# Token gather of a mixture-of-experts block: rows staged through HBM against quarter rows gathered straight to the DVE transpose, with the low part of h moved from POOL to DVE

## The chip, the cores and the metric

One Trainium2 chip, one core. The time is the device time of one execution in microseconds (us). Engines are named as the profile names them: PE (TensorE matmul), PEld (its weight loads), DVE (VectorE), ACT (ScalarE), POOL (GpSimd), SP (SyncE, which only issues DMAs here).

## The reference

Sixteen sequences of 256 tokens with 512 features go through a gated cross attention and then through a gated mixture of 8 experts with the two best experts of each token. Cut to what matters:

```python
x = x + tanh(g_xattn) * attention(layernorm(x), ctx, Wq, Wkv)
xn = layernorm(x)
probs = softmax(xn @ gate_w + gate_b, axis=1)          # over the tokens
vals, idx = top_k(probs, 2)
h = relu(xn @ w1[e] + b1[e]); h = relu(h @ w2[e] + b2[e]); y = relu(h @ w3[e] + b3[e])
v[e] = sum over the tokens of y * w_tok                # w_tok: vals where e was chosen, else 0
out = x + tanh(g_ffn) * (ind @ v)                      # ind: 1 where e was chosen
```

## The kernel before

All products are made in a split form: each operand is written as a high part (rounded to fp32r) and a low part (the rest), and PE adds three products, high x high, high x low and low x high (`split_product`, lines 1314 to 1323). So every operand needs one pass that writes the high part, on ACT, and one that subtracts it from the original, on DVE or POOL.

The attention and the gate run over the 16 sequences, up to about 400 us. Each token's two choices get a slot in a list sorted by expert; POOL scatters pairs (token number, weight) into `slot_pair` in HBM (`send_pairs`). Then the experts run over tiles of 352 slots of one expert. A table on the chip gives each tile's expert and first slot (`table`). There are 24 tiles here: the first (0 to 3) are interleaved with the end of the attention, and from tile 2 on a loop with a run-time count does the rest (`tile_pipeline`, lines 85 to 90: body(j) for j from 2, the last four tiles unrolled). In body(j) each engine has its own fixed order:

- PE (lines 1606 to 1619): layer 2 of tile j, layer 1 of tile j+1, layer 3 of tile j, each in two halves of 24 matmuls of 128x352.
- ACT (888 to 897): high part of w2 (third weights, `split_w(2, j)`), ReLU and high part of layer 2's result (`relu(1, j)`: per half two ReLUs to `h`, L837, and one copy to `h_hi`, L843), high part of the next w1 (`split_w(1, j+1)`), `relu(0, j+1)`, high part of the first weights (`split_w(0, j+2)`, L826) and of the activations (`et_high(j+2)`, L854).
- DVE (1272 to 1284): low parts of the three weights (`w_low`, L938, 128x2048), the transpose of the gathered rows (`transpose_blocks`, L1196), `weights_of` (L1213, L1214), the low part of the activations (L1202), and `weighted_sum(j)` (L1224 four times from PSUM, then L1229, L1232, L1236), which ends in the semaphore part_done.
- POOL (699 to 705): low part of h, `h_low(1, j)` and `h_low(0, j+1)` (L675, four instructions a tile), then `gather(j+3)`: three indirect DMAs (L665) of 128, 128 and 96 rows of 2 KB from the normalised activations `xn2_dram` to `xg`.
- SP (544 to 561): weight and bias loads (`load_w` loads only where the expert differs from the tile before), and for tile j+3 `store_rows` (L532, L533: `xg` to `rows_dram` in HBM), `load_idx(j+4)` (L491) and `load_quarters(j+3)` (L542: four DMAs from `rows_dram` to `xq`). All of it is one queue in this order, each entry behind its own waits.

`xq` holds 32-row blocks: partition q*32+b, block g holds quarter q of row g*32+b. The DVE transpose of 32x32 blocks then gives `et`, features on partitions and slots along the free dimension. Only tiles from BY_BLOCKS = 4 on go this way; PE transposes tiles 0 to 3 from `xg`. There is one `xq`, one `et` and one `et_hi`/`et_lo`. Layer 1 of tile m waits for the low parts of its weights and activations and for part_done of tile m-2 (line 1505), because it writes the PSUM banks that the weighted sum reads. Layer 3 waits for `h_lo` of layer 2, and layer 2 for `h_lo` of layer 1.

Of the kernel before, what the change touches and what calls it, by code (L numbers as in the profile page):

```python
# [71 lines left out]
NQ = P // QB  # L72
BY_BLOCKS = 4
# [24 lines left out]
def flamingo_block(nc, x, x_t, ctx_t, g_xattn, g_ffn, wq_t, wk_t, wv, gate_w, gate_b,  # L98
# [10 lines left out]
    rows_dram = nc.dram_tensor("rows_dram", (TILE, D), F32).ap()  # L109
# [4 lines left out]
    with ExitStack() as ctx:  # L114
# [124 lines left out]
        with ExitStack() as ph:  # L239
# [26 lines left out]
            et = alloc(ph, "et", [P, DC, TILE], F32)  # L266
            h_hi, h_lo = [h_hi0, h_hi1], [h_lo0, h_lo1]
# [81 lines left out]
        rows_out, xq_in, et_ready = sem("rows_out"), sem("xq_in"), sem("et_ready")  # L349
# [53 lines left out]
        def _(sp):  # L403
# [122 lines left out]
            def store_rows(m):  # L526
                need(sp, gathered, 16 * TH * (m + 1))
                wait_alone(sp, "sp")
                need(sp, xq_in, 16 * NQ * (m - BY_BLOCKS))
                wait_alone(sp, "sp")  # L530
                full = TILE // P
                sp.dma_start(rows_dram[0:full * P].rearrange("(c p) d -> p c d", p=P), xg[:, 0:full]).then_inc(rows_out, 16)  # L532
                sp.dma_start(rows_dram[full * P:], xg[0:TILE - full * P, full]).then_inc(rows_out, 16)  # L533

            def load_quarters(m):
                need(sp, rows_out, 32 * (m - BY_BLOCKS + 1))
                wait_alone(sp, "sp")
                need(sp, et_ready, m - BY_BLOCKS)
                wait_alone(sp, "sp")
                for q in range(NQ):  # L540
                    rows = rows_dram[:, q * P:(q + 1) * P].rearrange("(g b) d -> b g d", b=QB)
                    sp.dma_start(xq[q * QB:(q + 1) * QB], rows).then_inc(xq_in, 16)  # L542

            def tile(j, left):
# [23 lines left out]
            store_rows(BY_BLOCKS)  # L568
            load_quarters(BY_BLOCKS)
# [11 lines left out]
        def _(pool):  # L581
# [70 lines left out]
            def gather(m):  # L652
# [4 lines left out]
                if isinstance(m, int) and m <= BY_BLOCKS:  # L657
                    need(pool, te_done, TH * m)
                else:
                    need(pool, rows_out, 32 * (m - BY_BLOCKS))  # L660
                wait_alone(pool, "pool")

                rows = xn2_dram[0:KNOWN * S] if isinstance(m, int) and m < EARLY else xn2_dram
# [33 lines left out]
            gather(4)  # L697
# [214 lines left out]
        def _(dve):  # L912
# [280 lines left out]
            def transpose_blocks(m):  # L1193
                dve.wait_ge(xq_in, 16 * NQ * (m - BY_BLOCKS + 1))
                need(dve, et_his, TH * m)
                dve.transpose(et[:].rearrange("p k (g b) -> p g k b", b=QB),  # L1196
                              xq[:].rearrange("p g (i k) -> p g k i", k=DC)).then_inc(et_ready, 1)

            def et_low(m, chunks=range(TH)):
# [4 lines left out]
                for c in chunks:  # L1204
# [3 lines left out]
                        et_hi[:, :, a:a + n], et_los)  # L1208

# [474 lines left out]
```

## Time and profile before

| | |
|---|---|
| median of 3 runs | 947.28 us (940.92 to 947.80) |
| the profiled execution | 942.43 us |
| its span, first to last instruction | 940.3 us |
| granted TensorE clock, mean | 0.986 |
| busy share of PE, DVE, ACT, POOL | 97%, 70%, 52%, 47% |
| DMA: HBM read, written | 106.66 MB, 31.53 MB |

Busy shares are over the whole span. The matmuls are pipelined, so a PE that is busy all the time says that it is never without work, not how fast the work goes; how often a tile comes round is read from the starts of its matmuls. An engine other than PE matters where something that PE waits for is late. POOL's idle time is mostly waiting for ACT.

### The profile page before, as it was taken

The page shows a single profiled execution, that of the slowest core. Times are in us where ns is not written, and L with a number is a line of the kernel's source. Part 1 is how long each engine was busy: PE and PEld are TensorE (multiplying, and loading weights), DVE is VectorE, ACT ScalarE, POOL GpSimd, SP SyncE. Part 2 cuts the span into 40 slices and gives each one's busy share as a digit, 9 for nine tenths or more (in the row PEclk, how much of TensorE's full clock was granted, in tenths as well). Part 3 has the DMA queues.
Part 4 walks back from the last instruction along what each step waited for, and adds up shares of the span by engine and source line. Part 5 has one row for each costly group of instructions (what it writes and reads, how often), then busy time and mean ns, then how long its engine had stood idle before and what let it go on. Part 6 is the DMA issues. An engine that isn't in the chain of part 4 may idle for free.

```text
span 940.3 us, 18821 instructions
## 1 busy us (share of the span) xinstructions
PE 913.8 (97%) x5746; PEld 860.1 (91%) x5746; DVE 661.1 (70%) x1283; ACT 493.6 (52%) x690; POOL 446.0 (47%) x402
## 2 busy tenths in 40 slices
PE   9999999999999989999999999999999999999985
PEld 6989988889888879999999999999999999999981
DVE  5667778888778787966676756667676666676546
ACT  5444444454443367545555665556666566566421
POOL 4224444445444558653545454456545454544213
PEclk9999999999999999999999999999999999999995
DMA  6433332233322444546575778885464555554008
GB/s 236 157 110 117 108 117 90 89 112 111 123 78 68 108 135 116 137 110 183 155 192 166 206 219 245 238 242 163 120 189 152 138 167 153 138 171 152 17 16 357
DMA packets 91924, 138.67 MB, mean 147 GB/s; under 512 B 28528, under 2 KB 56944, under 8 KB 88688
## 3 DMA queue, kind: packets, MB, share of 16 engines
q1 hardware_dynamic: 84464, 120.86, 42.3%
q0 software_dynamic: 7424, 17.38, 6.3%
q8 instruction: 18, 0.29, 0.1%
q14 instruction: 18, 0.15, 0.1%
HBM read 106.66 MB, written 31.53 MB: 147 GB/s over the span
## 4 chain that ended last, share of the span: by engine, by line
PE 68%; issue 14%; POOL 7%; DVE 5%; SPq 2%; DMA 2%; ACT 1%; POOLq 0%; DVEq 0%; ACTq 0%
PE bank L1319 20%; PE bank L1320 20%; PE bank L1321 20%; POOL h_lo L675 4%; POOL xg L665 2%; DVE x_all L1309 2%; PE bank L1333 1%; DMA xg<-xn_dram,idx 1%; PE bank L1402 1%; PE bank L1443 1%; PE bank L1343 1%; SPq L464 1%; PE bank L1445 0%; DMA wb<-slot_pair 0%; POOL slot_pair L635 0%
## 5 line engine op out<-in xcount | busy, mean ns | idle before, releaser
L675 POOL TENSOR_TENSOR h_lo<-h,h_hi 128x704 fp32r<-128x704 f32 x96 | 183.6, 1916 | 252.0 <-ACT h_hi L843 251.9
L1319 PE MATMUL bank<-h_hi,w_hi 128*128 128x352 f32 x744 | 241.5, 325 | 1.1 <-issue 1.1
L1321 PE MATMUL bank<-h_hi,w_lo 128*128 128x352 f32 x744 | 240.1, 323 | 0.0
L1320 PE MATMUL bank<-h_lo,w_hi 128*128 128x352 f32 x744 | 239.1, 321 | 0.0
L938 DVE TENSOR_TENSOR w_lo<-w_raw,w_hi 128x2048 fp32r<-128x2048 f32 x72 | 170.0, 2362 | 98.2 <-ACT w_hi L826 92.3
L826 ACT ACTIVATE w_hi<-w_raw 128x2048 fp32r<-128x2048 f32 x72 | 137.5, 1909 | 89.9 <-DMA w_raw<-in_w 52.4
L837 ACT ACTIVATE h<-bank,bias 128x352 f32<-128x352 f32 x192 | 95.7, 550 | 123.9 <-PE bank L1321 120.3
L1319 PEld LDWEIGHTS bank<-h_hi,w_hi 128*128 128x128 f32 x744 | 139.8, 188 | 1.5 <-issue 1.4
L1320 PEld LDWEIGHTS bank<-h_lo,w_hi 128*128 128x128 f32 x744 | 139.7, 188 | 0.0
L1321 PEld LDWEIGHTS bank<-h_hi,w_lo 128*128 128x128 f32 x744 | 139.4, 187 | 0.0
L1319 PE MATMUL bank<-et_hi,w_hi 128*128 128x352 f32 x384 | 124.3, 324 | 4.7 <-DVE part L1229 3.3
L1320 PE MATMUL bank<-et_lo,w_hi 128*128 128x352 f32 x384 | 123.0, 320 | 0.0
L1321 PE MATMUL bank<-et_hi,w_lo 128*128 128x352 f32 x384 | 123.0, 320 | 0.0
L665 POOL DMA_INDIRECT xg<-xn_dram,idx x72 | 94.5, 1312 | 26.4 <-issue 16.7
L635 POOL DMA_INDIRECT slot_pair<-pair,slot_u x64 | 68.0, 1062 | 37.6 <-DVE pair L995 19.3
L843 ACT ACTIVATE h_hi<-h 128x704 fp32r<-128x704 f32 x96 | 76.2, 794 | 5.5 <-PE bank L1445 1.7
L1319 PEld LDWEIGHTS bank<-et_hi,w_hi 128*128 128x128 f32 x384 | 72.0, 188 | 6.0 <-issue 4.4
L1320 PEld LDWEIGHTS bank<-et_lo,w_hi 128*128 128x128 f32 x384 | 72.2, 188 | 0.0
L1321 PEld LDWEIGHTS bank<-et_hi,w_lo 128*128 128x128 f32 x384 | 72.0, 187 | 0.0
L602 POOL TENSOR_SCALAR rn<-mv 128x2 f32<-128x2 f32 x32 | 9.0, 281 | 130.5 <-DVE mv L935 130.4
L1319 PE MATMUL bank<-xt_hi,a_hi 128*128 128x256 f32 x240 | 69.1, 288 | 0.0
L1321 PE MATMUL bank<-xt_hi,a_lo 128*128 128x256 f32 x240 | 67.9, 283 | 0.0
(214 smaller groups left out, 1781.5 us busy)
## 6 DMA issues: line engine op xcount, KB each, us to landing
w_raw<-in_w SPq DMA_DIRECT2D x24, 1024.0 KB
xq<-rows_dram SPq DMA_DIRECT2D x80, 176.0 KB
w_raw<-in_w SPq DMA_DIRECT2D x48, 256.0 KB
rows_dram<-xg SPq DMA_DIRECT2D x20, 512.0 KB, 3.1
wb<-slot_pair SPq DMA_DIRECT2D x24, 352.0 KB
xt_raw<-in_x_t SPq DMA_DIRECT2D x16, 512.0 KB, 4.0
c_raw<-in_ctx_t SPq DMA_DIRECT2D x16, 512.0 KB
x_all<-in_x SPq DMA_DIRECT2D x16, 512.0 KB
```

Source lines behind the costliest of these rows:

```text
L464: sp.dma_start(w_raw[0][q * QB:(q + 1) * QB], rows).then_inc(w_in[0], 16)
L635: pool.indirect_dma_start(slot_pair, bass.IndirectOffsetOnAxis(ap=slot_u[:, k, n:n + 1], axis=0), pair[:, k, n], None).then_inc(pair_sent[ ...
L665: pool.indirect_dma_start(xg[0:n, c], None, rows, bass.IndirectOffsetOnAxis(ap=idx[0:n, c, 0:1], axis=0)).then_inc(gathered, 16)
L675: pool.tensor_tensor(h_lo[n][:, 2 * k:2 * k + 2], h[:, 2 * k:2 * k + 2], h_hi[n][:, 2 * k:2 * k + 2].bitcast(F32), ALU.subtract).then_inc( ...
L826: act.activation(w_hi[n][:], w_raw[n][:], ACT.Copy).then_inc(w_his[n], 1)
L837: act.activation(h[:, oc], layer_banks(n, m)[oc][:, 0:TILE], ACT.Relu, bias=bias[n][:, oc:oc + 1]).then_inc(relu_done[n], 1)
L843: act.activation(h_hi[n][:, 2 * k:2 * k + 2], h[:, 2 * k:2 * k + 2], ACT.Copy).then_inc(h_his[n], 1)
L938: dve.tensor_tensor(dst, src, hi.bitcast(F32), ALU.subtract).then_inc(done, 1)
L1309: dve.tensor_tensor(row, bank[n % 8][:], row, ALU.add).then_inc(res_dve, 1)
L1319: pe.matmul(out_ap, lh, rh, start=(i == 0), stop=False)
L1320: pe.matmul(out_ap, lh, rl, start=False, stop=False)
L1321: last = pe.matmul(out_ap, ll, rh, start=False, stop=(i == n - 1))
```

## The change

Two things are changed for tiles from 4 on.

1. The low part of h (`h_rest`) is written by DVE from tile 2 on (low parts that the loop body makes), between the weight low parts, instead of by POOL. POOL keeps those of the prologue.
2. `rows_dram` is gone, and with it `store_rows`, `load_quarters` and, for these tiles, `xg`. SP now loads, for each of the 128 partitions, the slot entries that it needs (`load_idx_pairs`: four DMAs, `idx_pair`); POOL turns token numbers into numbers of quarter rows, 4 x token + quarter, in one instruction, and then issues 11 indirect DMAs, each of 128 quarter rows of 512 bytes, straight to `xq[:, g]`. Partition q*32+b of block g now holds row b*11+g, so the transpose writes `et` with a step of 11 elements (44 bytes) where it wrote 32 neighbours before. POOL gathers a tile only when the transpose of the tile before has read `xq`.

```diff
+    xn2_quarters = xn2_dram.rearrange("t (q d) -> (t q) d", q=NQ)
...
+            def load_idx_pairs(m):
+                need(sp, idx_quarters, m - BY_BLOCKS)
                 wait_alone(sp, "sp")
+                r = sp.value_load(table[0:1, bass.ds(m, 1), 1:2], min_val=0, max_val=NSLOT - TILE)
                 for q in range(NQ):
+                    sp.dma_start(idx_pair[q * QB:(q + 1) * QB].rearrange("b g a -> b (g a)"),
+                                 slot_pair[bass.ds(r, TILE)].rearrange("(b g) a -> b (g a)", g=NG)).then_inc(idx_pair_in, 16)
...
-                if has_tile(3, left) and not isinstance(j, int):
-                    store_rows(j + 3)
+                if has_tile(3, left):
+                    load_w(0, j + 3)
                 if has_tile(4, left):
-                    load_idx(j + 4)
-                if has_tile(3, left):
-                    if not isinstance(j, int):
-                        load_quarters(j + 3)
-                    load_w(0, j + 3)
+                    load_idx_pairs(j + 4)
...
+            def gather_quarters(m):
+                pool.wait_ge(idx_pair_in, 16 * NQ * (m - BY_BLOCKS + 1))
+                wait_alone(pool, "pool")
+                need(pool, et_ready, m - BY_BLOCKS)
+                wait_alone(pool, "pool")
+                pool.tensor_scalar(idx_quarter[:], idx_pair[:, :, 0], float(NQ), quarter[:, 0:1], ALU.mult, ALU.add
+                                   ).then_inc(idx_quarters, 1)
+                pool.wait_ge(idx_quarters, m - BY_BLOCKS + 1)
+                wait_alone(pool, "pool")
+                rows = xn2_quarters[0:KNOWN * S * NQ] if isinstance(m, int) else xn2_quarters
+                for g in range(NG):
+                    pool.indirect_dma_start(xq[:, g], None, rows,
+                                            bass.IndirectOffsetOnAxis(ap=idx_quarter[:, g:g + 1], axis=0)
+                                            ).then_inc(xq_in, 16)
...
             def tile(j, left):
-                if has_tile(0, left):
-                    h_low(1, j)
-                if has_tile(1, left):
-                    h_low(0, j + 1)
                 if has_tile(3, left):
-                    gather(j + 3)
+                    gather_quarters(j + 3)
...
-                dve.transpose(et[:].rearrange("p k (g b) -> p g k b", b=QB),
+                dve.transpose(et[:].rearrange("p k (b g) -> p g k b", b=QB),
                               xq[:].rearrange("p g (i k) -> p g k i", k=DC)).then_inc(et_ready, 1)
...
+            def h_rest(n, m):
+                for k in range(2):
+                    dve.wait_ge(h_his[n], 2 * m + k + 1)
+                    low(h_lo[n][:, 2 * k:2 * k + 2], h[:, 2 * k:2 * k + 2], h_hi[n][:, 2 * k:2 * k + 2], h_los[n])
...
                 if has_tile(0, left):
                     w_low(2, j)
+                    h_rest(1, j)
                 if has_tile(1, left):
                     w_low(1, j + 1)
+                    h_rest(0, j + 1)
```

NG is 11 (TILE 352 by QB 32), NQ is 4 and TH is 3.

POOL in the loop over the tiles (xn_dram is `xn2_dram`). Before, one round of body(j), from the loop's entry to the gather:

```order
L87 ISA
L675 TENSOR_TENSOR h_lo<-h,h_hi 128x704
L674 REGISTER_ALU
L675 TENSOR_TENSOR h_lo<-h,h_hi 128x704
L674 ISA
L675 TENSOR_TENSOR h_lo<-h,h_hi 128x704
L674 REGISTER_ALU
L675 TENSOR_TENSOR h_lo<-h,h_hi 128x704
L41 ISA x2
L665 DMA xg<-xn_dram,idx 128x512 x2
L665 DMA xg<-xn_dram,idx 96x512
L87 ISA
```

Now the same round:

```order
L88 ISA
L41 REGISTER_ALU
L660 TENSOR_SCALAR idx_quarter<-idx_pair,quarter 128x11
L666 DMA xq<-xn_dram,idx_quarter 128x128 x11
L88 ISA
L88 COMPARE_AND_BRANCH
```

POOL's four subtractions are gone, and three indirect DMAs have become one small instruction and eleven indirect DMAs.

DVE in the loop, from the low part of the third weights to the low part of the activations. Before (w_lo here is the low part of weights 2, 1 and 0 in turn, bank the PSUM result of layer 3):

```order
L938 TENSOR_TENSOR w_lo<-w_raw,w_hi 128x2048
L1189 REGISTER_ALU
L938 TENSOR_TENSOR w_lo<-w_raw,w_hi 128x2048
L1194 ISA
L41 REGISTER_ALU
L1196 STREAM_TRANSPOSE et<-xq 128x11x4x32
L1211 REGISTER_ALU
L1213 TENSOR_SCALAR nb<-bias 128x4
L1214 TENSOR_REDUCE wsum<-wb 128x1
```

Now:

```order
L939 TENSOR_TENSOR w_lo<-w_raw,w_hi 128x2048
L1213 ISA
L939 TENSOR_TENSOR h_lo<-h,h_hi 128x704
L1213 REGISTER_ALU
L939 TENSOR_TENSOR h_lo<-h,h_hi 128x704
L1190 REGISTER_ALU
L939 TENSOR_TENSOR w_lo<-w_raw,w_hi 128x2048
L1213 ISA
L939 TENSOR_TENSOR h_lo<-h,h_hi 128x704
L1213 REGISTER_ALU
L939 TENSOR_TENSOR h_lo<-h,h_hi 128x704
L1195 ISA
```

The transpose, which in the round now is the next instruction of work, stands behind four more subtractions, each of which waits for its high part from ACT.

## Rows read from the trace of the kernel before

**Rows 1.** The page: the engines' busy time, and the chain that ended last.

```profile
PE 913.8 (97%) x5746; PEld 860.1 (91%) x5746; DVE 661.1 (70%) x1283; ACT 493.6 (52%) x690; POOL 446.0 (47%) x402
...
PE 68%; issue 14%; POOL 7%; DVE 5%; SPq 2%; DMA 2%; ACT 1%; POOLq 0%; DVEq 0%; ACTq 0%
```

**Rows 2.** Windows: stretch, its length, busy time of each engine, PEclk, DMA share.

```profile
440.00:900.00 460.00, 458.12 (x2856) 457.37 (x2857) 304.49 (x361) 273.21 (x313) 223.47 (x133) 1.00 0.58 166
```

**Rows 3.** Timeline of PE: start, duration, engine, line, operation, idle before and its releaser.

```profile
438.20 0.32 PE L1321 MATMUL bank<-h_hi,w_lo 128*128 128x352 f32 x1
440.32 0.40 PE L1319 MATMUL bank<-et_hi,w_hi 128*128 128x352 f32 x1 [1.79 <-DVE part L1229]
...
649.99 0.32 PE L1319 MATMUL bank<-et_hi,w_hi 128*128 128x352 f32 x1
...
673.05 0.32 PE L1319 MATMUL bank<-et_hi,w_hi 128*128 128x352 f32 x1
```

**Rows 4.** Groups of 420 to 930 us: count, busy us, mean ns, idle before.

```profile
L675 POOL TENSOR_TENSOR h_lo<-h,h_hi 128x704 fp32r<-128x704 f32 x84 | 159.8, 1905 | 239.3 <-ACT h_hi L843 239.3
...
L1196 DVE STREAM_TRANSPOSE et<-xq 128x1408 f32<-128x1408 f32 x20 | 54.8, 2738 | 15.7 <-DMA xq<-rows_dram 15.6
```

**Rows 5.** Timeline of POOL, indirect DMAs of five gathers.

```profile
402.54 2.86 POOL L665 DMA_INDIRECT xg<-xn_dram,idx  x1
...
546.76 2.85 POOL L665 DMA_INDIRECT xg<-xn_dram,idx  x1 [0.30 <-issue]
...
661.58 3.04 POOL L665 DMA_INDIRECT xg<-xn_dram,idx  x1
664.92 1.20 POOL L665 DMA_INDIRECT xg<-xn_dram,idx  x1 [0.30 <-issue]
666.43 0.92 POOL L665 DMA_INDIRECT xg<-xn_dram,idx  x1 [0.30 <-issue]
...
684.64 0.97 POOL L665 DMA_INDIRECT xg<-xn_dram,idx  x1 [0.16 <-issue]
```

**Rows 6.** Timeline of DVE, beside the gather at 661.58.

```profile
661.48 2.29 DVE L938 TENSOR_TENSOR w_lo<-w_raw,w_hi 128x2048 fp32r<-128x2048 f32 x1 [1.36 <-ACT w_hi L826]
663.69 1.62 DVE L1202 TENSOR_TENSOR et_lo<-et,et_hi 128x1408 fp32r<-128x1408 f32 x1
665.22 0.59 DVE L1224 SCALAR_TENSOR_TENSOR bank<-bank,nb,wb 128x352 f32<-128x352 f32 x1
...
668.53 0.19 DVE L1236 TENSOR_TENSOR v_sum<-v_sum,v_add 128x32 f32<-128x32 f32 x1
```

**Rows 7.** Timeline of DVE, tile 4's transpose and what follows.

```profile
430.39 2.70 DVE L1196 STREAM_TRANSPOSE et<-xq 128x1408 f32<-128x1408 f32 x1 [8.96 <-DMA xq<-rows_dram]
...
433.47 2.29 DVE L938 TENSOR_TENSOR w_lo<-w_raw,w_hi 128x2048 fp32r<-128x2048 f32 x1
```

**Rows 8.** Timeline of ACT, the last high part of layer 1, two tiles.

```profile
658.85 0.79 ACT L843 ACTIVATE h_hi<-h 128x704 fp32r<-128x704 f32 x1
...
424.19 0.79 ACT L843 ACTIVATE h_hi<-h 128x704 fp32r<-128x704 f32 x1
```

**Rows 9.** Timeline of SP's queue: stores that wait for a gather, and first weights' load.

```profile
555.58 0.39 SPq L532 DMA_DIRECT2D rows_dram<-xg  x1
...
563.17 2.91 SPq L464 DMA_DIRECT2D w_raw<-in_w  x4
...
669.88 0.39 SPq L532 DMA_DIRECT2D rows_dram<-xg  x1
```

**Rows 10.** Waits: engine, line, waited for, us in total, times, longest.

```profile
POOL h_lo L675 <- ACT h_hi L843: 251.9, 84, 10.4
...
ACT w_hi L826 <- DMA w_raw<-in_w: 52.4, 16, 5.8
...
PE bank L1319 <- DVE part L1229: 3.3, 3, 1.8
```

**Rows 11.** A small POOL instruction, from the page's groups.

```profile
L602 POOL TENSOR_SCALAR rn<-mv 128x2 f32<-128x2 f32 x32 | 9.0, 281 | 130.5 <-DVE mv L935 130.4
```

More of the change, by code:

```diff
@@ L72 @@
 NQ = P // QB
+NG = TILE // QB
 BY_BLOCKS = 4
@@ L266, in flamingo_block @@
             et = alloc(ph, "et", [P, DC, TILE], F32)
+            idx_pair = alloc(ph, "idx_pair", [P, NG, 2], U32)
+            idx_quarter = alloc(ph, "idx_quarter", [P, NG], U32)
+            quarter = alloc(ph, "quarter", [P, 1], F32)
             h_hi, h_lo = [h_hi0, h_hi1], [h_lo0, h_lo1]
@@ L348, in flamingo_block @@
         idx_in, wb_in, gathered = sem("idx_in"), sem("wb_in"), sem("gathered")
-        rows_out, xq_in, et_ready = sem("rows_out"), sem("xq_in"), sem("et_ready")
+        xq_in, et_ready = sem("xq_in"), sem("et_ready")
+        idx_pair_in, idx_quarters, quarter_set = sem("idx_pair_in"), sem("idx_quarters"), sem("quarter_set")
         te_done, et_his, et_los = sem("te_done"), sem("et_his"), sem("et_los")
@@ L524, in _ @@
             load_idx(3)
-            def store_rows(m):
-                need(sp, gathered, 16 * TH * (m + 1))
+            def load_idx_pairs(m):
+                need(sp, idx_quarters, m - BY_BLOCKS)
                 wait_alone(sp, "sp")
[L529 to L539, printed above, removed]
+                r = sp.value_load(table[0:1, bass.ds(m, 1), 1:2], min_val=0, max_val=NSLOT - TILE)
                 for q in range(NQ):
-                    rows = rows_dram[:, q * P:(q + 1) * P].rearrange("(g b) d -> b g d", b=QB)
-                    sp.dma_start(xq[q * QB:(q + 1) * QB], rows).then_inc(xq_in, 16)
+                    sp.dma_start(idx_pair[q * QB:(q + 1) * QB].rearrange("b g a -> b (g a)"),
+                                 slot_pair[bass.ds(r, TILE)].rearrange("(b g) a -> b (g a)", g=NG)).then_inc(idx_pair_in, 16)
             def tile(j, left):
@@ L567, in _ @@
                 sp.wait_ge(pair_sent[n], 16 * RC * TOPK * sends_by_end(n))
-            store_rows(BY_BLOCKS)
-            load_quarters(BY_BLOCKS)
             tile_pipeline(sp, tile, tiles)
@@ L656, in gather @@
                     pool.wait_ge(xn2_ready, RC * KNOWN + 1)
[L657 to L660, printed above, removed]
+                need(pool, te_done, TH * m)
                 wait_alone(pool, "pool")
-                rows = xn2_dram[0:KNOWN * S] if isinstance(m, int) and m < EARLY else xn2_dram
+                rows = xn2_dram[0:KNOWN * S]
                 for c, (_, n) in enumerate(CHUNKS):
@@ L696, in _ @@
             h_low(0, 2)
-            gather(4)
+            pool.wait_ge(h_los[0], 2 * 3)
+            for q in range(NQ):
+                pool.memset(quarter[q * QB:(q + 1) * QB], float(q)).then_inc(quarter_set, 1)
+                pool.wait_ge(quarter_set, q + 1)
+            gather_quarters(BY_BLOCKS)
             def tile(j, left):
-                if has_tile(0, left):
-                    h_low(1, j)
-                if has_tile(1, left):
-                    h_low(0, j + 1)
                 if has_tile(3, left):
-                    gather(j + 3)
+                    gather_quarters(j + 3)
             tiles = tiles_in_use(pool)
@@ L1193, in transpose_blocks @@
             def transpose_blocks(m):
-                dve.wait_ge(xq_in, 16 * NQ * (m - BY_BLOCKS + 1))
+                dve.wait_ge(xq_in, 16 * NG * (m - BY_BLOCKS + 1))
                 need(dve, et_his, TH * m)
-                dve.transpose(et[:].rearrange("p k (g b) -> p g k b", b=QB),
+                dve.transpose(et[:].rearrange("p k (b g) -> p g k b", b=QB),
                               xq[:].rearrange("p g (i k) -> p g k i", k=DC)).then_inc(et_ready, 1)
```

1 line of the change is left out of this document (removed).

## The prediction

> **What bounds the kernel now.** I read the page first. PE is busy 97% of the span and holds 68% of the chain that ended last; no other engine holds more than 7% [rows 1]. Then the windows: in the 460 us from 440 to 900, where the loop over the tiles runs, PE is busy for 458.1 [rows 2]. Then PE's timeline. From the first layer 1 matmul of one tile to that of the next is 673.05 - 649.99 = 23.06 us, 144 matmuls without a stall [rows 3]. So the loop costs PE's own work and nothing can make it faster than 23.06 a tile, since the change leaves PE's instructions as they are. What is to be won in it is PE's idle time: 460 - 458.1 = 1.9 us, and 440.32 - 438.20 less one spacing of 0.16, some 2.0 us, while PE waits for part_done at the start of the loop [rows 2, 3]. The waits agree (3.3 us for the sum L1229, three times) [rows 10]. That is 4 us in all, at most.
>
> The large wait of POOL, 252 us for h_hi [rows 10], is idle time of an engine that PE never waits for in the loop. So the question is what the change makes late. Each tile now has one chain that leads back to itself: the transpose on DVE frees `xq`, POOL gathers the next tile into it, the data land, DVE transposes. If a round of that takes over 23.06, it, and no longer PE, sets the time of a tile.
>
> **Part 1, the low part of h on DVE.** Four subtractions of 128x704 leave POOL (1.9 us each [rows 4]) and come to DVE. DVE takes 2.29 for 2048 elements and 1.62 for 1408 [rows 6], so 1.05 ns an element and 0.14 fixed: 0.88 for 704, 3.5 us a tile. DVE has a share of some 304.5/460 = 66% here, 15.3 us of 23.06 [rows 2], so 18.8, 82%: it fits by its sum. Its order matters more. The high part of layer 1's second half ends at 659.64, that is 9.65 after layer 1 begins [rows 3, 8]; the transpose stands behind its subtraction, so it can't begin before 9.65 + 0.88 = 10.5. It ends at 13.3. After a transpose DVE needs about 7.0 until part_done: 0.4 to the weights' low part [rows 7], then 2.2, 1.5 and 3.0 at the starts of [rows 6]. So part_done comes at 20.3 in a round where layer 1 needs it at 23.06: a cover of 2.8 us. PE loses nothing by part 1 alone.
>
> **Part 2, what goes.** The stores, the reload and their queue places on SP go. That is hidden work, except at two places. Tile 4's transpose waited 8.96 us for `xq` until 430.39 [rows 7]; the new gather of tile 4 starts where the old one did, at 402.54 [rows 5], needs some 20, and the transpose then stands behind the last high part of tile 3 (424.98 [rows 8]), so it begins near 426: the first stall of 2.0 goes. And the first weights' load stood behind the row copies (563.17 [rows 9]); it now follows its own condition, so most of the 52.4 us of ACT's waits for `w_raw` [rows 10] and the other 1.9 us of PE's stalls should go. Gain: 4 us.
>
> **Part 2, what comes: the round of the gather.** An indirect DMA costs POOL 0.97 us, with 0.30 before the next [rows 5], and the 96-row one hardly less than those of 128, so I take it that indices are paid for and not bytes. Eleven: 11 x 0.96 + 10 x 0.30 = 13.6. Before them stands the index arithmetic: 0.28 for a small POOL instruction [rows 11] and two handovers, 0.6 together.
>
> But the first DMA at 661.58 took 3.04. The subtraction w_lo had begun 0.10 before it and ended at 663.77; the DMA ended 0.84 after that. The next, begun at 664.92, ended 0.81 after et_lo (665.31), and the one beside the sums from PSUM took its plain 0.92 [rows 5, 6]. So an indirect DMA that starts while DVE subtracts SBUF from SBUF stands until the subtraction ends, and then needs 0.84 more.
>
> The Trainium skill bears on this (SBUF — State Buffer, section "Who interferes with whom"): a DVE instruction with two SBUF inputs contends with a GpSimd instruction that reads SBUF, but it infers that descriptor generation is not held up by `tensor_tensor`. The trace agrees with the first, if reading the indices counts, and not with the inference: by that a round would be 18.4 us.
>
> Now walk one round, time 0 at the end of a transpose. DVE: w_low 0.4 to 2.6, et_low to 4.1, the sums (PSUM, harmless) to 7.6, w_low to 9.9, two h_low to 11.5, w_low to 13.7, h_low to 14.5, and the last h_low from 16.8 to 17.7 when its high part is there. POOL: the first DMA starts at 0.6, stands behind w_low, ends 3.4 (+1.9 over its 0.96); the second ends 4.95 (+0.3); two run free; the fifth meets w_low at 7.8 and ends 10.7 (+2.0); the sixth meets h_low (+0.3); the seventh w_low (+0.9); two free; the tenth meets the last h_low (+0.2); the eleventh ends at 19.8. Stalls: 5.6 us. Landing: after the gather that ended at 667.35 SP stored at 669.88, 2.5 later [rows 5, 9], with 2 KB rows; with a quarter of the bytes I take 1.5 (bounds 0.5 and 2.5). The transpose costs 2.74 [rows 4]. Round: 0.6 + 13.6 + 5.6 + 1.5 + 2.7 = 24.0 us, 0.94 over PE's 23.06.
>
> There are 19 such rounds (tile 4's transpose to tile 23's): 17.9 us, less the cover of 2.8. Where weights are loaded, the landing is later: after the gather that ended at 549.61 SP stored only at 555.58, 6.0 against 2.5 [rows 5, 9]. The last gathers of a tile meet the load of the second weights in perhaps a third of the rounds, half of that delay at most in the mean: 4 us (0 to 12).
>
> **Sum** against the profiled execution (942.43, of which 2.1 lie outside its span): 942.4 - 4 + 17.9 - 2.8 + 4 = 957.5. Its time is 4.9 under the median of the runs; against that it would be 962.4. I forecast 960.
>
> **Rivals.**
> - *The round fits under PE.* With 0.5 for landing the round is 23.0; with an index instruction that lets the first DMA start within 0.4 us, ahead of w_low, some 1.3 us less. At 23.06 or less PE stays the bound, and only the gain of 4 us is left: 938.4, 0.4% faster than before. It decides below 0.94 us less than my round, which the landing alone can give. For it: the data are small. Against it: the stalls in [rows 5], and every weight load adds to the landing. A round without any stall (18.4 us) would end at the same 938.4; it has 0.03 of the 0.24 below, since the rows show stalls. (It is what the Trainium skill's inference of part 2 would make of it, SBUF — State Buffer, "Who interferes with whom".) It is the case on the other side, not slower than before.
> - *The transpose gets dearer.* 1408 elements cost a plain subtraction 1.62 [rows 6] and the transpose 2.74 [rows 4]. The transpose reads with a step of 16 bytes, the subtraction with neighbours; 1.12 us is what that step may cost. Now the write has a step of 44 bytes. If it costs as much again, a round is 25.1: 942.4 - 4 + 19 x 2.06 - 2.8 + 4 = 978.7. Against it: reading and writing may overlap, then it is nothing, which I take. The Trainium skill (SBUF — State Buffer, section "Door 1: The DMA port swizzle") says that SBUF lines are 16 bytes long and each access that crosses to a new line pays; it gives no price. The read side in this trace agrees; of a write no row shows it.
> - *POOL's index arithmetic is caught too.* It reads SBUF about 0.2 us after the transpose, w_low begins at 0.4. If it comes second, it stands until 2.6 and the first DMA with it behind et_low: one DMA and its gap later, 1.26 a round. 942.4 - 4 + 19 x 2.20 - 2.8 + 4 = 981.4.
>
> **Chances.** My case 0.52, the round that fits 0.24, the two dearer ones together 0.20, the rest 0.04 (eleven DMAs in flight hold one another up; or an ordering gain that I don't see). A measurement here tells about 1% from no change. My case covers some 946 to 972, of which 0.07 lies within 1%; the fitting round is within 1% but for 0.03; the dearer ones are slower. That gives faster 0.04, same 0.28, slower 0.68. Range: 938 for the round that fits, 988 for a dearer one with a little more contention; above lie both together and runaway cases.
>
> **What would show it.** In the changed profile: PE's period from tile 5 on, 24.0 where I say 23.06 otherwise, with the idle time ahead of L1319 on the et operands and released by the sum (part); an idle DVE ahead of the transpose for xq of some 3 to 4 us a tile; indirect DMAs of 0.96 with four or five a tile of 1.2 to 2.9; the transpose at 2.74; POOL's first DMA of a tile 0.6 after the transpose; no wait of ACT for first weights. The forecast is wrong if PE's loop has no stall, if the DMAs with long durations are rare, or if the transpose takes over 3 us.

## The result, and the profile after

The changed kernel takes 997.7 us (median of 5 runs, 994.96 to 1001.24) where the kernel before, beside it, takes 943.5 (5 runs): ratio 1.057, interval 1.053 to 1.061. It is slower, as forecast, but by 54 us and not by 17: the time lies outside the range of 938 to 988. The profiled execution took 994.96, its span 993.2.

The page of the changed kernel, engines, chain, and the three groups that belong to the gather:

```profile
PE 930.4 (94%) x5746; PEld 873.6 (88%) x5746; DVE 715.6 (72%) x1369; ACT 490.8 (49%) x690; POOL 535.6 (54%) x500
...
PE 38%; POOL 27%; issue 14%; DVE 10%; DMA 8%; ACT 1%; SPq 0%; POOLq 0%; DVEq 0%; ACTq 0%
POOL xq L666 21%; PE bank L1327 11%; PE bank L1328 10%; PE bank L1329 10%; DMA xq<-xn_dram,idx_quarter 6%; DVE et L1197 5%; POOL idx_quarter L660 4%; DVE x_all L1317 2%; PE bank L1341 1%; PE bank L1410 1%; DMA xg<-xn_dram,idx 1%; PE bank L1451 1%; DVE w_lo L939 1%; DMA idx<-slot_pair 1%; POOL xg L651 1%
...
L666 POOL DMA_INDIRECT xq<-xn_dram,idx_quarter x220 | 285.6, 1298 | 80.3 <-issue 63.7
...
L1197 DVE STREAM_TRANSPOSE et<-xq 128x1408 f32<-128x1408 f32 x20 | 56.9, 2843 | 90.0 <-DMA xq<-xn_dram,idx_quarter 90.0
...
L660 POOL TENSOR_SCALAR idx_quarter<-idx_pair,quarter 128x11 uint32<-128x11 uint32 x20 | 47.7, 2385 | 106.0 <-DVE et L1197 105.6
```

By busy share nothing has changed hands: PE still stands first with 94%. The chain says otherwise: PE's part fell from 68% [rows 1] to 38%, and POOL's gather, its landing, the transpose and the index arithmetic hold 21 + 6 + 5 + 4 = 36%. The windows show the same stretch of the loop as [rows 2], and the waits those of [rows 10]:

```profile
440.00:900.00 460.00, 422.77 (x2530) 418.56 (x2529) 311.18 (x379) 241.79 (x281) 292.16 (x210) 0.96 0.38 106
```

```profile
POOL idx_quarter L660 <- DVE et L1197: 94.2, 17, 7.1
DVE et L1197 <- DMA xq<-xn_dram,idx_quarter: 85.0, 18, 7.1
...
PE bank L1327 <- DVE part L1235: 37.2, 16, 4.4
```

PE was busy for 458.12 of these 460 us before and is now for 422.77, with 2530 matmuls instead of 2856. All its idle time, 37.2 us, is spent on part_done, in 16 stalls. POOL and DVE wait for each other in turn, which is what the chain that leads back to itself looks like in a table of waits. The 52.4 us that ACT waited for first weights are gone.

One round of the gather, in POOL's timeline and then in DVE's (start, length, what; in brackets the idle time before and its releaser):

```profile
640.95 2.44 POOL L660 TENSOR_SCALAR idx_quarter<-idx_pair,quarter 128x11 uint32<-128x11 uint32 x1 [7.07 <-DVE et L1197]
644.19 1.52 POOL L666 DMA_INDIRECT xq<-xn_dram,idx_quarter  x1 [0.81 <-POOL idx_quarter L660]
646.02 0.94 POOL L666 DMA_INDIRECT xq<-xn_dram,idx_quarter  x1 [0.31 <-issue]
...
648.51 3.06 POOL L666 DMA_INDIRECT xq<-xn_dram,idx_quarter  x1 [0.30 <-issue]
651.88 1.30 POOL L666 DMA_INDIRECT xq<-xn_dram,idx_quarter  x1 [0.30 <-issue]
653.49 1.90 POOL L666 DMA_INDIRECT xq<-xn_dram,idx_quarter  x1 [0.30 <-issue]
...
661.21 0.94 POOL L666 DMA_INDIRECT xq<-xn_dram,idx_quarter  x1 [0.30 <-issue]
```

```profile
637.91 2.83 DVE L1197 STREAM_TRANSPOSE et<-xq 128x1408 f32<-128x1408 f32 x1 [4.85 <-DMA xq<-xn_dram,idx_quarter]
...
641.02 2.29 DVE L939 TENSOR_TENSOR w_lo<-w_raw,w_hi 128x2048 fp32r<-128x2048 f32 x1
643.22 1.63 DVE L1203 TENSOR_TENSOR et_lo<-et,et_hi 128x1408 fp32r<-128x1408 f32 x1
...
648.47 2.29 DVE L939 TENSOR_TENSOR w_lo<-w_raw,w_hi 128x2048 fp32r<-128x2048 f32 x1 [0.20 <-issue]
650.67 1.69 DVE L939 TENSOR_TENSOR h_lo<-h,h_hi 128x704 fp32r<-128x704 f32 x2
652.28 2.29 DVE L939 TENSOR_TENSOR w_lo<-w_raw,w_hi 128x2048 fp32r<-128x2048 f32 x1
...
663.80 2.85 DVE L1197 STREAM_TRANSPOSE et<-xq 128x1408 f32<-128x1408 f32 x1 [3.71 <-DMA xq<-xn_dram,idx_quarter]
```

Lay the two side by side. The index arithmetic begins 0.21 after the transpose ended (640.74) and 0.07 before w_lo, yet it ends at 643.39, 0.08 after w_lo. The first DMA comes 0.81 later and stands behind et_lo, which ends at 644.85, until 645.71. The DMA of 648.51 begins 0.04 after the next w_lo, which ends at 650.76, and it ends 0.81 later; those of 651.88 and 653.49 end 0.82 after h_lo (652.36) and w_lo (654.57). The data of the last one, ended at 662.15, release the transpose at 663.80, 1.65 later.

The mean round is (923.9 - 425.4)/19 = 26.24 us, from tile 4's transpose to tile 23's. Taken apart on the same two timelines, in the mean of the rounds: 0.21 to wake POOL, 2.44 index arithmetic, 0.81 to the first DMA, 14.32 in the eleven DMAs (220 of them with a mean of 1298 ns), 3.21 between them, 2.41 landing and 2.84 transpose.

PE's timeline at the start of that tile's layer 1, and windows of the same stretch (us, busy time and instructions of PE, PEld, DVE, ACT and POOL, granted clock, DMA share, GB/s):

```profile
645.39 0.32 PE L1329 MATMUL bank<-h_hi,w_lo 128*128 128x352 f32 x1
647.87 0.40 PE L1327 MATMUL bank<-et_hi,w_hi 128*128 128x352 f32 x1 [2.16 <-DVE part L1235]
...
649.23 0.50 PE L1329 MATMUL bank<-et_hi,w_lo 128*128 128x352 f32 x1
649.53 0.50 PE L1327 MATMUL bank<-et_hi,w_hi 128*128 128x352 f32 x1
```

```profile
649.00:652.60 3.60, 3.60 (x15) 3.60 (x14) 3.60 (x4) 0.38 (x1) 3.29 (x2) 0.53 0.47 115
652.60:657.00 4.40, 4.40 (x30) 4.40 (x29) 2.86 (x2) 1.79 (x3) 3.79 (x3) 1.00 0.82 281
```

After a stall of 2.2 us PE ran some microseconds at a granted clock near 0.5, its level of 1.2 GHz, with 0.30 from one matmul to the next instead of 0.16. Whether that costs time is asked below.

### The profile page after: what moved, and what is told of

The parts are those of the page before. It is cut to its first block, busy times and chain, and to the rows that moved or that the text cites. A ratio compares the mean times of both kernels' runs of the same rounds, so it can differ in the third digit from the quotient of the medians.

```text
span 993.2 us, 18765 instructions
## 1 busy us (share of the span) xinstructions
PE 930.4 (94%) x5746; PEld 873.6 (88%) x5746; DVE 715.6 (72%) x1369; ACT 490.8 (49%) x690; POOL 535.6 (54%) x500
## 4 chain that ended last, share of the span: by engine, by line
PE 38%; POOL 27%; issue 14%; DVE 10%; DMA 8%; ACT 1%; SPq 0%; POOLq 0%; DVEq 0%; ACTq 0%
POOL xq L666 21%; PE bank L1327 11%; PE bank L1328 10%; PE bank L1329 10%; DMA xq<-xn_dram,idx_quarter 6%; DVE et L1197 5%; POOL idx_quarter L660 4%; DVE x_all L1317 2%; PE bank L1341 1%; PE bank L1410 1%; DMA xg<-xn_dram,idx 1%; PE bank L1451 1%; DVE w_lo L939 1%; DMA idx<-slot_pair 1%; POOL xg L651 1%
## 5 line engine op out<-in xcount | busy, mean ns | idle before, releaser
L666 POOL DMA_INDIRECT xq<-xn_dram,idx_quarter x220 | 285.6, 1298 | 80.3 <-issue 63.7
L1327 PE MATMUL bank<-et_hi,w_hi 128*128 128x352 f32 x384 | 131.8, 343 | 40.9 <-DVE part L1235 39.5
L1328 PE MATMUL bank<-et_lo,w_hi 128*128 128x352 f32 x384 | 128.9, 336 | 0.0
L1329 PE MATMUL bank<-et_hi,w_lo 128*128 128x352 f32 x384 | 128.7, 335 | 0.0
L939 DVE TENSOR_TENSOR h_lo<-h,h_hi 128x704 fp32r<-128x704 f32 x86 | 74.7, 887 | 70.5 <-ACT h_hi L844 70.4
L1197 DVE STREAM_TRANSPOSE et<-xq 128x1408 f32<-128x1408 f32 x20 | 56.9, 2843 | 90.0 <-DMA xq<-xn_dram,idx_quarter 90.0
L1327 PEld LDWEIGHTS bank<-et_hi,w_hi 128*128 128x128 f32 x384 | 77.0, 200 | 45.8 <-issue 44.1
L660 POOL TENSOR_SCALAR idx_quarter<-idx_pair,quarter 128x11 uint32<-128x11 uint32 x20 | 47.7, 2385 | 106.0 <-DVE et L1197 105.6
L855 ACT ACTIVATE et_hi<-et 128x1408 fp32r<-128x1408 f32 x20 | 27.8, 1389 | 131.1 <-DVE et L1197 131.1
L1328 PEld LDWEIGHTS bank<-et_lo,w_hi 128*128 128x128 f32 x384 | 77.3, 201 | 0.0
```

Source lines behind the costliest of these rows:

```text
L660: pool.tensor_scalar(idx_quarter[:], idx_pair[:, :, 0], float(NQ), quarter[:, 0:1], ALU.mult, ALU.add).then_inc(idx_quarters, 1)
L666: pool.indirect_dma_start(xq[:, g], None, rows, bass.IndirectOffsetOnAxis(ap=idx_quarter[:, g:g + 1], axis=0)).then_inc(xq_in, 16)
L855: act.activation(et_hi[:], et[:], ACT.Copy).then_inc(et_his, TH)
L939: dve.tensor_tensor(dst, src, hi.bitcast(F32), ALU.subtract).then_inc(done, 1)
L1197: dve.transpose(et[:].rearrange("p k (b g) -> p g k b", b=QB), xq[:].rearrange("p g (i k) -> p g k i", k=DC)).then_inc(et_ready, 1)
L1327: pe.matmul(out_ap, lh, rh, start=(i == 0), stop=False)
```

## The experiments

The theory after this result: the round through the one `xq` sets the time of a tile, as forecast; it is 26.24 and not 24.0 because the index arithmetic is caught behind DVE's subtraction and because the data land late beside weight loads. Rivals: DVE's fuller queue (part 1), the clock that PE loses in its stalls, the strided write of the transpose.

**Part 1 alone.** The kernel before, with the low part of h on DVE; nothing else.

```diff
 POOL, tile(j):
-                if has_tile(0, left):
-                    h_low(1, j)
-                if has_tile(1, left):
-                    h_low(0, j + 1)
 DVE, tile(j):
                     w_low(2, j)
+                    h_rest(1, j)
...
                     w_low(1, j + 1)
+                    h_rest(0, j + 1)
```

> The kernel before with part 1 of the change alone: DVE writes the low part of h in the loop, the rows still go through HBM. Theory (the round transpose, gather, landing, transpose through the one xq is what costs the 54 us): part 1 costs nothing, PE's loop stays at 23.06 us a tile, 938 to 946 us, the same as before. Rival (DVE's fuller queue, 3.6 us more a tile and the transpose behind it, makes part_done late): 24 us a tile or more, 960 to 1000 us.

Measured: 943.4 us against 944.7, ratio 0.998 (0.997 to 1.000). PE is busy for 457.3 of the 460 us:

```profile
440.00:900.00 460.00, 457.32 (x2847) 457.35 (x2848) 355.41 (x449) 277.34 (x316) 66.63 (x54) 1.00 0.60 166
```

DVE does 355 us of work there instead of 304 [rows 2], and the time doesn't notice. Part 1 costs nothing, and all the loss belongs to part 2.

**Part 2 alone.** The changed kernel, with the low part of h back on POOL, ahead of the gather.

> The changed kernel with part 2 alone: POOL writes the low part of h again, in its order before the gather of each tile. Theory (POOL's order is now a chain: the two low parts of a tile, which lie 13.4 us apart by PE's pace, and then a gather of 21 us, in which no low part is made while PE waits for one): 31 to 34 us a tile, 1100 to 1160 us. Rival (POOL was idle for half of the time, there is room for both): near 998 us.

Measured: 1019.7 us, one run: far below the 1100 to 1160 of the theory and over the 998 of the rival. In the stretch 440 to 900 the subtraction sits on POOL again, now between gathers, and its result is late for PE and ACT (the tile h_lo: count, shortest, median and longest in ns, first and last start; then who waited for it):

```profile
L676 POOL TENSOR_TENSOR h_lo<-h,h_hi x68: 1672/1708/3417, 447.6 to 886.6; 128x704 fp32r<-128x704 f32 x68
...
  ACT h L842: 49.8, 11
  PE bank L1329: 30.7, 8
```

The mean round is (938.8 - 427.1)/19 = 26.93, only 0.7 longer than in the changed kernel, but single rounds go from 22.6 to 32.4 us. DVE waits for `xq` in 9 of the 19 rounds only, 37.9 us in all, where it waits in all 19 of the changed kernel, 90.0 us. So in the other rounds the ring through `xq` is not what ends last; the late h_lo is the wait that the profile shows. I had put all four subtractions into each round at full length. That they fit in part into the time in which POOL waited anyway (7.1 us in the round above) is my reading and not shown. The rounds make 13 of the 24 us between the two profiled executions, and 9 come after the last transpose. Part 1 is thus what makes part 2 bearable: it is worth 1019.7 - 997.7 = 22 us there, by one run, and nothing by itself.

**The index arithmetic ahead of the wait.** The changed kernel, with the arithmetic done before POOL waits for the transpose. The DMAs of the gather before may still read the indices, so there are two buffers of them and two tiles a loop body.

```diff
-                need(pool, et_ready, m - BY_BLOCKS)
-                wait_alone(pool, "pool")
-                pool.tensor_scalar(idx_quarter[:], idx_pair[:, :, 0], float(NQ), quarter[:, 0:1], ALU.mult, ALU.add
+                pool.tensor_scalar(idx_quarter[par][:], idx_pair[:, :, 0], float(NQ), quarter[:, 0:1], ALU.mult, ALU.add
                                    ).then_inc(idx_quarters, 1)
                 pool.wait_ge(idx_quarters, m - BY_BLOCKS + 1)
                 wait_alone(pool, "pool")
+                need(pool, et_ready, m - BY_BLOCKS)
+                wait_alone(pool, "pool")
```

> The changed kernel with the index arithmetic ahead of POOL's wait for the transpose (two idx_quarter buffers, and a loop whose body holds two tiles). In the changed kernel the first DMA of a tile ends 4.97 us after the transpose, because the arithmetic stands 2.44 us behind the low part of the weights and then 0.81 us go by. Theory: now the first DMA starts some 0.4 us after the transpose, meets the low part of the weights and ends at 3.4, the second ends behind et_low at 4.95, so one DMA and its gap are won, 1.25 us a round: 19 x 1.25 = 24, so 974 us. Rival (all of the 3.46 us of wake, arithmetic and handover is won): the round falls under PE's 23.06, 940 us. Rival (the round isn't the bound): 998 us.

Measured: 978.4 us (one of four runs took 4051 and is left out), ratio 1.036 (1.032 to 1.040): 19 us gained. The two tiles of gather and transpose, and the arithmetic:

```profile
L1198 DVE STREAM_TRANSPOSE et<-xq x20: 2824/2846/2866, 426.7 to 906.3; 128x1408 f32<-128x1408 f32 x20
...
L659 POOL TENSOR_SCALAR idx_quarter<-idx_pair,quarter x20: 287/288/1458, 404.3 to 879.6; 128x11 uint32<-128x11 uint32 x20
```

```profile
735.90 2.63 POOL L667 DMA_INDIRECT xq<-xn_dram,idx_quarter  x1 [4.93 <-DVE et L1198]
738.84 1.18 POOL L667 DMA_INDIRECT xq<-xn_dram,idx_quarter  x1 [0.31 <-issue]
```

The arithmetic takes 0.29 when no DVE subtraction runs beside it. The round is (906.3 - 426.7)/19 = 25.24, 1.0 shorter and not 3.2: the first DMA starts 0.8 after the transpose and now takes the stall behind w_low itself (2.63), and the second stands behind et_low. In the mean of the rounds 2.65 us go before the first DMA, and 1.36 come back in the DMAs (15.68 for 14.32) and 0.28 in the landing (2.69 for 2.41). The expectation had the first DMA start 0.4 after the transpose. The 0.81 is still there although the arithmetic has long been done, so it is what POOL takes from its release to an indirect DMA, and not a handover from the arithmetic. With w_low 0.3 after the transpose, the DMA can't be ahead of it.

**The loop body of two tiles only**, the control to the last run.

> Control: the changed kernel, only with a loop whose body holds two tiles, as in the kernels e3 and e6. Theory: the form of the loop costs and brings nothing, 995 to 1001 us, rounds of 26.2 us. Rival (the shorter way through the loop's branch is what helped e3 and e6): clearly under 995.

Measured: 999.8 us, one run, mean round (928.3 - 429.1)/19 = 26.27. The loop's form brings nothing; the 19 us belong to the arithmetic.

**No weight loads in the loop.** SP only counts the semaphore up; so all tiles of the loop use the weights of the first ones.

```diff
-                with sp.If(e != previous):
-                    load()
-                with sp.Else():
-                    sp.sem_inc(w_in[n], W_IN[n])
+                if isinstance(m, int):
...
+                else:
+                    sp.sem_inc(w_in[n], W_IN[n])
```

> The changed kernel without any load of weights in the loop over the tiles (the tiles from the loop on use weights that are already there, so that part of the computation is changed; every engine does the same work). Theory: the last gather lands 1.65 us after its DMA's end in every tile instead of 2.45 in the mean, so 0.8 us a round go, 15 us: 983 us. Rival (weight traffic has no part in it, the late landings have another reason): 998 us, landings of 3 to 4 us stay in some ten of the twenty tiles.

Measured: 985.3 us, ratio 1.044 (1.040 to 1.047). The tile `xq` of that kernel:

```profile
L1200 DVE STREAM_TRANSPOSE et<-xq x20: 2823/2842/2867, 426.3 to 913.7; 128x1408 f32<-128x1408 f32 x20
```

Round (913.7 - 426.3)/19 = 25.65. The mean landing is 1.67 there, 2.41 in the changed kernel. In the latter nine landings of the 19 rounds took 2.2 to 4.0 us, and 177 to 292 GB/s moved while they lasted (0.4 to 0.9 MB); the other ten took 1.65 to 1.90, with 35 to 40 GB/s. The windows of two landings of the changed kernel, the one at 634 and that at 662, differ in what moved on the DMA engines (the last two columns, share and GB/s) and hardly in anything else:

```profile
633.90:637.90 4.00, 4.00 (x26) 4.00 (x25) 0.00 (x0) 0.05 (x1) 0.00 (x0) 1.00 0.46 177
662.20:663.80 1.60, 1.60 (x11) 1.60 (x10) 0.00 (x0) 0.00 (x0) 0.00 (x0) 1.00 0.16 41
```

**Both together**, to see whether the two terms are separate times.

> The changed kernel with the two edits of e3 and e4 together: the index arithmetic stands ahead of the wait for the transpose (two buffers of it, two tiles a loop body), and no weights are loaded in the loop (the computation is left wrong in that part: the three weight matrices of the first tiles serve all tiles). Theory: the forecast's step was right in kind and its two terms before the first DMA and on landing were too small; with both terms near what was forecast, the mean round is 26.24 - 1.0 (e3) - 0.6 (e4) = 24.6 us, so 19 rounds give 997.7 - 19 x 1.6 = 967 us (960 to 972), close to the 960 forecast. Rival (the two gains are the same time, since the stall of the first DMA behind w_low takes what landing gives back): no better than the better of the two alone, 978.

Measured: 956.0 us, ratio 1.013 (1.011 to 1.016), 4 us below the 960 to 972 of the theory and far from the rival's 978. Its windows, and its transposes:

```profile
440.00:900.00 460.00, 447.62 (x2767) 444.20 (x2766) 341.03 (x421) 268.56 (x311) 293.14 (x223) 1.00 0.18 46
```

```profile
L1201 DVE STREAM_TRANSPOSE et<-xq x20: 2822/2846/2880, 426.8 to 884.7; 128x1408 f32<-128x1408 f32 x20
```

The round is (884.7 - 426.8)/19 = 24.10: the gains of 1.0 and 0.6 add up, and 0.5 more comes with them. About half of that is in the landings: with the arithmetic ahead alone they were at 2.69, later than before, and here they are at 1.64. Link by link the round is 0.81 to the first DMA, 18.8 for the DMAs and their gaps, 1.64 landing and 2.85 transpose, where the forecast had 0.6, 19.2, 1.5 and 2.7. With the two terms near what was forecast, round (24.0) and time (957.5 to 960) come out as forecast too. The clock in this stretch is 1.00 where it was 0.96 before.

**DVE's long subtractions cut short.** The changed kernel, where DVE reads and writes only 32 of the 2048 columns for each low part of the weights in the loop; the rest stays that of the first tiles, so that part of the products is stale.

```diff
-                low(w_lo[n][:], w_raw[n][:], w_hi[n][:], w_los[n])
+                part = slice(0, DC) if isinstance(m, int) else slice(0, 1)
+                width = D if isinstance(m, int) else 32
+                low(w_lo[n][:, part, 0:width], w_raw[n][:, part, 0:width], w_hi[n][:, part, 0:width], w_los[n])
```

> The changed kernel, but in the loop over the tiles DVE writes only 32 of the 2048 columns of each low part of the weights (the rest of the computation's low parts is left out). Theory (POOL is held up by DVE's subtractions of SBUF from SBUF): the index arithmetic falls from 2.44 to about 1, the eleven DMAs from 14.3 to 11 to 12 us in sum, the round without PE would be 0.2 + 1 + 0.8 + 11.6 + 3.1 + 2.4 + 2.8 = 22, so PE is the bound again, 938 to 950 us. Rival (the long indirect DMAs come from something else, the DMA engines for instance): sums of 14 us stay and the time stays above 980.

Measured: 1071.3 us, one run, and a plain miss. POOL's durations went the theory's way, and somewhat further (0.41 for the arithmetic, 11 x 0.99 = 10.9 for the DMAs):

```profile
L666 POOL DMA_INDIRECT xq<-xn_dram,idx_quarter x220 | 218.3, 992 | 80.2 <-issue 64.0
...
L660 POOL TENSOR_SCALAR idx_quarter<-idx_pair,quarter 128x11 uint32<-128x11 uint32 x20 | 8.1, 407 | 276.8 <-DVE et L1199 276.5
```

But the round is (997.7 - 433.7)/19 = 29.7, since something else stops PE. Its timeline in one layer 1, and the windows around it:

```profile
661.01 0.32 PE L1331 MATMUL bank<-et_hi,w_lo 128*128 128x352 f32 x1
661.57 0.32 PE L1329 MATMUL bank<-et_hi,w_hi 128*128 128x352 f32 x1 [0.24 <-issue]
662.31 0.40 PE L1330 MATMUL bank<-et_lo,w_hi 128*128 128x352 f32 x1 [0.42 <-issue]
664.39 0.45 PE L1331 MATMUL bank<-et_hi,w_lo 128*128 128x352 f32 x1 [1.68 <-issue]
666.51 0.45 PE L1329 MATMUL bank<-et_hi,w_hi 128*128 128x352 f32 x1 [1.66 <-issue]
```

```profile
655.00:661.00 6.00, 6.00 (x39) 6.00 (x39) 2.14 (x8) 0.00 (x0) 4.57 (x5) 1.00 0.98 206
661.00:667.00 6.00, 1.95 (x7) 0.79 (x5) 0.89 (x1) 1.79 (x3) 3.85 (x4) 0.77 0.22 56
```

Single matmuls in the middle of a group, which wait for no semaphore that the profile shows, start 0.6 to 2.1 us apart. It lasts 3 to 7 us in nearly every round, and then the clock is at its lower level too; layer 1 takes 15.2 us (660.22 to 675.42) instead of 7.7. In this round weights were loaded at 206 GB/s until just before, but that is not a condition of the stops. In nine rounds between 440 and 990 no weight load was issued in the 8 us before layer 1, and they are there too. One of them, the window and PE's next stop:

```profile
882.00:890.00 8.00, 8.00 (x52) 8.00 (x51) 4.94 (x13) 3.67 (x4) 6.17 (x7) 1.00 0.18 43
```

```profile
893.21 0.32 PE L1329 MATMUL bank<-et_hi,w_hi 128*128 128x352 f32 x1 [0.96 <-issue]
```

Nor are the short subtractions a condition: in the kernel with part 2 alone, where they have their full length, six rounds have two such stops each, of 0.4 to 1.1 us:

```profile
606.42 0.40 PE L1330 MATMUL bank<-et_lo,w_hi 128*128 128x352 f32 x1 [0.55 <-issue]
607.83 0.32 PE L1329 MATMUL bank<-et_hi,w_hi 128*128 128x352 f32 x1 [0.85 <-issue]
```

The queues that load code moved nothing from 440 to 900 in the kernel with the short subtractions, so as far as the trace tells PE did not wait for code there. Two more kernels ask what these stops hang on.

**The same without weight loads.**

> e8 (short writes of the weights' low parts, one xq) without any weight load in the loop; the weights are stale. It asks whether the loads, which in e8 start earlier and run at 200 GB/s just before TensorE stops, are behind TensorE's stops in layer 1. Theory A (loads): no stops, round at PE's 23.06, 938 to 945 us. Theory B (not the loads): stops of 5 to 7 us a tile remain, about 1,060 us.

Measured: 938.3 us, one run. No stops, and none of PE's other stalls:

```profile
440.00:900.00 460.00, 460.00 (x2874) 460.00 (x2874) 235.36 (x437) 277.99 (x317) 217.19 (x221) 1.00 0.18 46
```

So without any load in the loop the stops are gone, though the gather begins in the same place, 8.3 us before layer 1 in both kernels. How that goes with the stops in rounds without a load, one above, is open; both kernels ran once. And here is what the one-buffer round is without its two disturbers: it fits under PE's 23.06 with room to spare (0.21 + 0.35 + 0.81 + 11.5 + 3.2 on POOL, 2.87 transpose and a landing of 1.65, taken from above, are 20.6; the rest is DVE's own order). Eleven DMAs, index arithmetic, one `xq` and the strided transpose are all still there, and the time is that of the first rival, 938.4.

**Two buffers of quarters.** The changed kernel with a second place for the gathered quarters, in the space of `xg`, which is free once tile 3 is transposed; indices in two buffers as above. The gather of tile m then waits for the transpose of tile m-2 and not of m-1.

```diff
+            xqs = [xq0[:], xg[:].rearrange("p c d -> p (c d)")[:, 0:NG * P].rearrange("p (g e) -> p g e", g=NG)]
...
-                need(pool, et_ready, m - BY_BLOCKS)
+                need(pool, et_ready, m - BY_BLOCKS - 1)
...
-                    pool.indirect_dma_start(xq[:, g], None, rows,
+                    pool.indirect_dma_start(xqs[par][:, g], None, rows,
```

> The changed kernel with two xq buffers (the second lies in xg, which is free by then), two idx_quarter buffers, the gather waiting for the transpose of the tile before the last, and a loop whose body holds two tiles. Theory: the chain from a transpose to the next is broken, POOL needs about 0.2 + 2.4 + 0.8 + 17.5 = 21 us a tile, less than PE's 23.06, so PE is the bound again: 938 to 945 us. Rival (eleven indirect DMAs are too many for POOL or for the DMA engines whatever waits for them): 24 us a tile or more, 960 us and up. Rival (DVE's queue is what is late): near 998 us.

Measured: 938.3 us (5 runs), ratio 0.993 (0.991 to 0.996) against the kernel before, 59 us faster than the changed one. It computes all that the kernel before does. The index arithmetic is ahead of the wait here too, which alone gave 978.4; the other 40 us are the second buffer's.

```profile
440.00:900.00 460.00, 460.00 (x2875) 460.00 (x2874) 352.94 (x438) 278.25 (x318) 308.10 (x218) 1.00 0.40 110
```

The long DMAs are still there (up to 4.12 us, 1.37 in the mean where the changed kernel has 1.30), and the weight loads too. PE has no idle time. The stalls cost nothing once no chain leads through them.

**Two buffers and the short writes.**

> e6 (two buffers of gathered quarters) with e8's edit: DVE writes only 32 of the 2048 columns of each weight's low part in the loop, so the low parts of the weights are stale there. It asks whether TensorE's stops in the middle of layer 1 (e8: 5 to 7 us a tile, with no wait behind them) come with the short writes and the quick gather alone. Theory A (they come from the gather's phase against layer 1 in e8, since e6 has none): no such stops, 936 to 941 us. Theory B (they come with a gather of 11 DMAs in 14 us without a stall, whenever it meets layer 1): stops in most rounds, over 960 us.

Measured: 938.3 us, one run, PE busy for all 460 us, no stops. So of the three kernels with short writes the one with one buffer and loads has the stops, and taking away either the loads or the single buffer takes them away, by one run each. By what mechanism they hold PE is open.

**Part 1 with the first weights' load moved up on SP.** The kernel with part 1 alone, `load_w(0, j + 3)` ahead of `store_rows`.

> The kernel before with part 1 (low part of h on DVE) and SP's load of the first weights ahead of the stores of the rows, rows still through HBM. Theory: the stalls of PE where the expert changes go, the one of 2 to 3.6 us at the start of the loop stays, since tile 4's rows come no earlier: 938 to 943 us, 0.1 to 0.5% under the kernel before. Rival (the first weights' wait now holds the stores back and xq comes late): 945 to 960 us.

Measured: 942.9 us against 944.8, ratio 0.997 (0.995 to 1.000), PE busy for 459.4 of 460. What part 2 was to win on SP's queue can be had without it, and it is within the noise.

## Why the prediction was right in kind and wrong in size

**What bounds the kernel, the bound of 23.06.** Right. The three kernels in which the round fits (two buffers, with and without short writes, and short writes without loads) end at 938.3, where 938.4 stood for that case: PE's own work less the 4 us of its stalls. That it agrees to 0.1 us is luck: the 938.4 starts from one execution of 942.4, and against the medians of the kernel before that ran beside them the gain is 5.7 to 6.4 us.

**Part 1 costs nothing.** Right, shown by itself (0.998), and it holds in the changed kernel too: the transpose at 425.4 stands where I put it (near 426).

**What goes.** Right: ACT's 52.4 us of waits and PE's stall at 438 are gone. (In the changed kernel PE's stalls then come back another way, 37.2 us of them.)

**"0.6 together" before the first DMA.** This is the step that failed first. It measured 0.21 + 2.44 + 0.81 = 3.46. I had the reader of SBUF 0.2 us after the transpose and w_low at 0.4 and took the first for safe; w_low came at 0.28, and the arithmetic, at 0.21, was caught all the same. The handover to the first DMA, 0.81, was also more than I had for both handovers and the arithmetic together. Against that stands a relief: the first DMA now starts after w_low and meets et_low only, 1.52 us in the mean where I had 2.8, and the second runs free, so DMAs and gaps cost 14.32 + 3.21 = 17.5 and not 13.6 + 5.6 = 19.2. Net +2.86 - 1.67 = +1.19 a round. The third rival had said 1.26, and it was the true case; I had given it, with the dearer transpose, 0.20. The run with the arithmetic moved ahead gives back 1.0 of it.

**"Landing 1.5", and "perhaps a third of the rounds" for 4 us.** The landing without loads is 1.65, near the 1.5. But nine rounds of 19 met a load and landed 1.5 us later in their mean (3.18, against 1.65), and the mean over all is 2.41. This is the second step that failed, in its size: (2.41 - 1.5) x 19 = 17 us came where I had 4. Of them 3 are the 1.65 for my 1.5 and 14 the loads, which is over even my bound of 12: nearly half of the rounds met a load, and not a third.

**The transpose.** 2.84 and not 2.74 for a write with a step of 44 bytes; the rival with 1.12 more falls.

**The sum, redone with the measured round**: 942.4 - 4 + 19 x (26.24 - 23.06) - 2.8 = 996.0, where 995.0 was measured. The same line gives 977.0 for a round of 25.24 (the profiled execution took 977.8), 984.8 for 25.65 (986.3) and 955.4 for 24.10 (956.0). So the form of the sum held over 40 us; it does not for the kernel with part 2 alone, where other waits set some rounds (1009 for 26.93, measured 1019.7). In the changed kernel it was right, and two of its terms were too small: +1.19, and 0.91 less the 0.21 a round that the 4 us stood for, and +0.10 for the transpose make 2.0 a round, 38 us, which with the 957.5 gives 995.

**The clock.** I had no term for it, and none is missing. The sum leaves it out and still fits within 1.5 us, with a mean granted clock of 0.96 in the stretch as with 1.00. PE's lower level comes after its waits (2.16 us idle, then the matmuls at 0.30 spacing). That the slow matmuls fall into time in which PE would have waited for the next round anyway is argued and not shown by a run; for it speaks that DVE, when it has done all that PE's results give it, still waits for `xq` in every round, 90.0 us in all. How far it would matter where PE is again the bound is not shown here.

**The range.** It ended at 988 because I let the dearer cases come one at a time. Yet the caught arithmetic, the landing and the contention lie on one chain in every round, so they add: 981.4, with 12 for 4 of contention, is 989 already.

## What to carry to other kernels

A chain that goes from engine to engine and back to a single buffer has to be summed link by link and compared with the bound's period, and the handovers and landings that look like nothing (0.8, 1.65) count in every round. Where such a round is near the period, a second buffer can be worth more than shorter links: here the two links shortened together still left 956.0, and the second buffer, with 938.3, made stalls of 3 to 4 us and late landings harmless at once. When links share a cause or a chain, the upper end of a range has to hold their sum, and not only the largest of them.

## What the runs showed of the hardware that I had not expected

- A POOL instruction on 128x11 integers took 0.29 us alone and 2.44 beside a DVE subtraction of two SBUF operands, although by the records it began 0.07 before the subtraction (POOL's times in a profile are rough): the earlier start did not save it. The Trainium skill (SBUF — State Buffer, section "Who interferes with whom") says that the one to issue second blocks until the first has finished. The waiting until 0.08 after the end agrees; the order of the two records here does not, if starts in the profile are taken for the order of issue.
- An indirect DMA took 0.94 us when free and up to 3.06 beside w_low, and in the round shown such DMAs ended 0.81 to 0.86 after the subtraction. So the inference in the same section of the Trainium skill (SBUF — State Buffer), that `tensor_tensor` leaves descriptor generation alone, does not carry over to these DMAs; whether they are held in reading their indices or in writing descriptors no run shows. With the subtractions of the weights cut to 32 columns their mean fell from 1.30 to 0.99 us.
- Before an indirect DMA passed 0.81 us from what released it, be it POOL's own arithmetic or the end of a DVE transpose; POOL's arithmetic started 0.21 after that end. From one indirect DMA to the next passed 0.30.
- A gather of 512 byte pieces landed 1.65 us after its last DMA instruction, and up to 4.0 beside weight loads that moved 177 to 292 GB/s.
- PE was stopped in the middle of a layer for 3 to 7 us a tile with no wait in the profile, in a kernel with weight loads in the loop and the one-buffer gather, in rounds with a load just before (206 GB/s) and without one (43 GB/s). Without any loads, or with two buffers, it was not. Each of these kernels ran once, and the cause is open.
